# Edge counts made already turned, by ten small products a chunk, with rings of three one-hot pairs

## The reference

```python
cond = silu(emb @ f_w1 + f_b1) @ f_w2 + f_b2          # 1250 x 16, from sin/cos of a noise level
for i in range(4):
    y = cond_layer_norm(x, cond, ...)                  # scale and bias from cond
    q, k, v = y @ wq + bq, y @ wk + bk, y @ wv + bv    # 4 heads of 128
    scores = einsum('ehd,ehd->eh', q[src], k[dst])     # one score an edge and head
    out = segment_sum(softmax_over_src(scores) * v[dst], src)
    x = x + out @ wo + bo
    x = x + relu(cond_layer_norm(x, cond, ...) @ m_w1 + m_b1) @ m_w2 + m_b2
# graph convolution: h = (x @ W), normalised by sqrt of the degrees of both ends, summed over edges, twice
```

## Time and profile before

| what | us |
|---|---|
| median of 3 runs | 1870.88 |
| lowest and highest of the 3 | 1868.85, 1871.59 |
| the profiled execution | 1871.84 |
| its span in the trace | 1870.1 |
| PE busy, of the span | 1810.0 (97%) |
| PEld busy | 1575.5 (84%) |
| DVE busy | 1382.6 (74%) |
| ACT busy | 826.5 (44%) |
| POOL busy | 453.8 (24%) |

### The profile page before, as it was taken

The page is one execution under the profiler, slowest core; times in us unless marked ns, Lnnn a source line. Parts: engine busy times, 40 slices in busy tenths (PEclk is TensorE's granted clock), DMA queues, the critical chain, the costliest instruction groups (busy, mean ns, idle before and its releaser), DMA issues. The chain is left out here.

```text
span 1870.1 us, 33910 instructions
## 1 busy us (share of the span) xinstructions
PE 1810.0 (97%) x11814; PEld 1575.5 (84%) x11814; DVE 1382.6 (74%) x2847; ACT 826.5 (44%) x1613; POOL 453.8 (24%) x547
## 2 busy tenths in 40 slices
PE   6988999999999999999999999999999999999999
PEld 4656988999789889998898899988998999887877
DVE  8996668888875588888754988888549888885431
ACT  1552465555432255554322545544226545536220
POOL 2000333112341341113413411125134111262000
PEclk9999999999999999999999999999999999999999
DMA  4213462110300111113011211040112110522001
GB/s 143 55 41 79 141 176 91 38 43 27 123 24 34 58 42 39 38 31 124 4 54 42 58 38 38 27 128 1 46 50 61 38 38 27 142 72 55 1 1 55
DMA packets 50755, 108.43 MB, mean 58 GB/s; under 512 B 18170, under 2 KB 18222, under 8 KB 50640
## 3 DMA queue, kind: packets, MB, share of 16 engines
q1 hardware_dynamic: 50608, 106.87, 19.7%
q0 software_dynamic: 32, 0.03, 0.0%
HBM read 83.62 MB, written 23.25 MB: 57 GB/s over the span
## 5 line engine op out<-in xcount | busy, mean ns | idle before, releaser
L876 ACT ACTIVATE PT<-ps 125x500 fp32r<-125x500 f32 (+1 forms) x480 | 214.3, 520 | 315.1 <-PE ps L1790 315.1
L1690 PE MATMUL ps<-PT,V 125*128 125x250 f32 x2400 | 313.2, 284 | 1.7 <-DVE PT L1288 1.7
L1690 PE MATMUL ps<-kT,qg 128*125 128x512 f32 (+1 forms) x1440 | 302.1, 354 | 6.3 <-DVE nmx L1272 5.6
L1690 PEld LDWEIGHTS ps<-kT,qg 128*125 128x125 f32 x1440 | 245.4, 186 | 56.0 <-issue 6.9
L1690 PEld LDWEIGHTS ps<-PT,V 125*128 125x128 f32 x2400 | 289.6, 190 | 2.9 <-DVE PT L1288 2.9
L1288 DVE TENSOR_TENSOR PT<-ps,PT 125x500 fp32r<-125x500 f32 (+1 forms) x480 | 253.1, 582 | 2.1 <-ACT PT L876 1.7
L1272 DVE CUSTOM_DVE_ANT_0 SB<-ps,bt 125x1250 f32<-125x1250 f32 x140 | 203.9, 1457 | 47.4 <-PE ps L1690 44.6
L1790 PE MATMUL ps<-ident,pbuf 125*125 125x125 f32 x1600 | 202.2, 273 | 9.9 <-DVE PT L1288 4.0
L1790 PEld LDWEIGHTS ps<-ident,pbuf 125*125 125x125 f32 x1600 | 187.2, 189 | 13.6 <-issue 8.8
L870 ACT ACTIVATE pbuf<-SB,nmx 125x1250 f32<-125x1250 f32 x140 | 188.1, 1344 | 12.1 <-DVE nmx L1272 10.4
L1281 DVE TENSOR_SCALAR pbuf<-pbuf,rden 125x1250 f32<-125x1250 f32 x160 | 150.1, 938 | 5.6
(11 more groups left out here) (246 smaller groups left out, 2811.6 us busy)
## 6 DMA issues: line engine op xcount, KB each, us to landing
bt<-edge_bias_scratch SPq DMA_DIRECT2D x40, 546.9 KB
q_scratch<-qc SPq DMA_DIRECT2D x16, 500.0 KB, 2.6
qc<-q_scratch SPq DMA_DIRECT2D x16, 500.0 KB, 4.8
counts_scratch<-cblk SPq DMA_DIRECT2D x10, 546.9 KB
c_rows<-counts_scratch SPq DMA_DIRECT2D x10, 546.9 KB
edge_bias_scratch<-b_rows SPq DMA_DIRECT2D x10, 546.9 KB
counts<-counts_scratch SPq DMA_DIRECT2D x10, 546.9 KB
wm<-in_L_gnn_wo_dram SPq DMA_DIRECT2D x4, 1024.0 KB, 8.6
```

Source lines behind the costliest of these rows:

```text
L876: sc.activation(PT[:, h % 2, 0, a:b, u * T:(u + 1) * T], ps_T[0:T, i, 0:(b - a) * T].rearrange("p (t n) -> p t n", n=T), ACT.Copy).then_in ...
L1690: e = mm(out_, lhs(a), rhs(b), start=start and i == 0, stop=stop and i == 2)
```

## The change

The roles of the two one-hots are swapped. For each chunk, ten products have a 125-column block of `oh_src` as the stationary operand and `oh_dst` (125 columns) as the moving one, so the sums arrive already turned: sources on the partitions, destinations of the tile along the row. `ct`, the turning, its two banks and the semaphores `ct` and `ct_t` go. `oh_src` gets two more columns of ones, so the last block of each chunk has 126 rows and its last one sums to the number of edges of each destination; ScalarE copies it to `degT` and SyncE sends it through DRAM to `deg` (a store of 5 KB in the counting stage, and a load of 1250 single elements in the first layer). The rings hold three slots each and loops go in threes (21 chunks where a tile meets 19, 18 elsewhere). `split_wa_lo(1)` and `split_wa_lo(0)` leave the counting loop: the first goes after `yT_low(0)`, the second after `front_mod` in VectorE's first `project`. Several early buffers move to other places. `condition(i)` now waits for the evicted result before it, not for the turning.

```diff
-SIX = 6
-ECP = EC + SIX
+TRIO = 3
+ECP = EC + TRIO
...
+            sp.dma_start(deg_dram[0:1, :], degT[T:T + 1, :, :].rearrange("o t p -> o (t p)")).then_inc(s["deg_ld"], 16)
             for i in range(2):
                 sp.wait_ge(s[f"cnt_out{i}"], NT * 16)
...
                     for i in range(2):
                         sp.wait_ge(s[f"bst_out{i}"], NT * 16)
+                    sp.wait_ge(s["deg_ld"], 16)
+                    sp.dma_start(deg[:, :], deg_dram.rearrange("o (t p) -> p (o t)", p=T), allow_slow_non_contiguous=True).then_inc(s["deg_ld"], 16)
                     load_o(l)
...
+            g.memset(oh_src[:, :, N:N + 2], 1.0).then_inc(s["consts"], 1)
...
             for i in range(2):
                 pool.wait_ge(s[f"cnt_out{i}"], NT * 16)
+            pool.wait_ge(s["deg_ld"], 16)
...
-            def count_out(t):
+            def blocks_out(t):
                 act.wait_ge(s["ct_mm"], t + 1)
                 if t >= 2:
-                    act.wait_ge(s["ct_t"], AHEAD + 3 * (t - 1))
-                sc.activation(ct[t % 2], psf[0:T, ACC[t % 2]:ACC[t % 2] + N], ACT.Copy, accum_out=deg[:, t:t + 1]).then_inc(s["ct"], 1)
...
+                o = ACC[t % 2]
+                sc.activation(degT[96:T + 1, t, :], psf[96:T + 1, o + 1024 + T:o + 1024 + 2 * T], ACT.Copy)
                 for p, (a, b) in enumerate(PIECES):
-                    act.wait_ge(s["ct_t"], AHEAD + (t * 3 + p + 1))
-                    sc.activation(cblk[t % 2][:, a:b, :], ps_q[0:T, p % 2, 0:(b - a) * T].rearrange("p (t n) -> p t n", n=T),
+                    sc.activation(cblk[t % 2][:, a:b, :], psf[0:T, o + 512 * p:o + 512 * p + (b - a) * T].rearrange("p (t n) -> p t n", n=T),
                                   ACT.Copy).then_inc(s["ct_e"], 1)
...
-                with dve.Fori(0, sixes) as i:
+                with dve.Fori(0, trios) as i:
...
-                    for b in range(SIX):
-                        slot = ring * SIX + b
+                    for b in range(TRIO):
+                        slot = ring * TRIO + b
...
                 front_mod(f)
                 if first and n:
                     edge_bias(2 * n - 1)
+                if first and n == 0:
+                    split_wa_lo(0)
                 k_out(l, n)
...
-                if t in (4, 5, 6):
-                    split_wa_lo(6 - t)
+                if t == 4:
+                    split_wa_lo(2)
...
             yT_low(0, yTb)
+            split_wa_lo(1)
             layer(0, False, True)
...
-                    pe.wait_ge(s["ct"], AHEAD + t - 1)
+                    pe.wait_ge(s["ct_e"], AHEAD + 3 * (t - 1))
...
-                    for q in range(SIX):
-                        slot = ring * SIX + q
+                    for q in range(TRIO):
+                        slot = ring * TRIO + q
                         pe.wait_ge(s[f"onehot{ring}"], done + (q + 1))
-                        for a, b in COLS:
-                            e = mm(psf[0:T, o + a:o + b], oh_dst[:, slot, 0:T], oh_src[:, slot, a:b], start=False, stop=False,
-                                   skip_group_check=True)
+                        for p, (a, b) in enumerate(PIECES):
+                            for m in range(a, b):
+                                r = T + (m == NT - 1)
+                                e = mm(psf[0:r, o + 512 * p + (m - a) * T:o + 512 * p + (m - a + 1) * T],
+                                       oh_src[:, slot, m * T:m * T + r], oh_dst[:, slot, 0:T], start=False, stop=False, skip_group_check=True)
                         e.then_inc(s[f"oh_used{ring}"], 1)
...
-            pe.wait_ge(s["ct"], AHEAD + NT)
+            pe.wait_ge(s["ct_e"], AHEAD + 3 * NT)
             scale_bias(0, 0)
-            turn_counts(NT - 2, 2)
-            for p in range(3):
-                turn_counts(NT - 1, p)
             turn_y(0)
```

More of the change, by code:

```diff
@@ L229, in build @@
         cblk = [blocks(f"cblk{i}", [T, NT, T]) for i in range(2)]
-        ct = [blocks(f"ct{i}", [T, N])[:, :] for i in range(2)]
+        degT = blocks("degT", [T + 1, NT, T])
         in_wm = packer(r_wm, r_wm + 4 * 3 * KD * D)
@@ L471, in _ @@
             for ring in range(2):
-                pool.sem_inc(s[f"oh_used{ring}"], SIX)
+                pool.sem_inc(s[f"oh_used{ring}"], TRIO)
             g.memset(ident[:, :], 0.0).then_inc(s["ident"], 1)
@@ L1115, in one_hots @@
                                         edgeT[:, 1, bass.ds(chunk0 + b, 1)], None, ALU.is_equal)
-                        v.tensor_scalar(oh_src[:, slot, :], iota16[:, :], edgeT[:, 0, bass.ds(chunk0 + b, 1)], None,
+                        v.tensor_scalar(oh_src[:, slot, 0:N], iota16[:, :], edgeT[:, 0, bass.ds(chunk0 + b, 1)], None,
                                         ALU.is_equal).then_inc(s[f"onehot{ring}"], 1)
@@ L1615, in open_counts @@
             def open_counts(t):
                 if t >= 2:
-                    pe.wait_ge(s["ct"], AHEAD + t - 1)
-                for a, b in COLS:
-                    mm(psf[0:T, ACC[t % 2] + a:ACC[t % 2] + b], zeros16[:, 0:T], zeros16[:, 0:b - a], start=True, stop=False,
-                       skip_group_check=True)
-            def count_tile(t, sixes, before):
+                    pe.wait_ge(s["ct_e"], AHEAD + 3 * (t - 1))
+                for p, (a, b) in enumerate(PIECES):
+                    mm(psf[0:T + 1, ACC[t % 2] + 512 * p:ACC[t % 2] + 512 * p + (b - a) * T], zeros16[:, 0:T + 1], zeros16[:, 0:(b - a) * T],
+                       start=True, stop=False, skip_group_check=True)
@@ L1625, in count_tile @@
+            def count_tile(t, trios, before):
                 ring, o = t % 2, ACC[t % 2]
[L1626 to L1629 removed]
+                with pe.Fori(0, trios) as i:
+                    done = pe.snap((before + i) * TRIO)
+                    for q in range(TRIO):
+                        slot = ring * TRIO + q
                         pe.wait_ge(s[f"onehot{ring}"], done + (q + 1))
[L1631 to L1633 removed]
+                        for p, (a, b) in enumerate(PIECES):
+                            for m in range(a, b):
+                                r = T + (m == NT - 1)
+                                e = mm(psf[0:r, o + 512 * p + (m - a) * T:o + 512 * p + (m - a + 1) * T],
+                                       oh_src[:, slot, m * T:m * T + r], oh_dst[:, slot, 0:T], start=False, stop=False, skip_group_check=True)
@@ L1634, in count_tile @@
                         e.then_inc(s[f"oh_used{ring}"], 1)
                 following = trips(t + 1) if t + 1 < NT else None
-                for a, b in COLS:
-                    e = mm(psf[0:T, o + a:o + a + 2], zeros16[:, 0:T], zeros16[:, 0:2], start=False, stop=True, skip_group_check=True)
+                for p in range(3):
+                    e = mm(psf[0:T + 1, o + 512 * p:o + 512 * p + 2], zeros16[:, 0:T + 1], zeros16[:, 0:2], start=False, stop=True,
+                           skip_group_check=True)
@@ L1638, in count_tile @@
                 e.then_inc(s["ct_mm"], 1)
                 return following
-            def turn_counts(t, p):
-                a, b = PIECES[p]
-                if p == 0:
-                    pe.wait_ge(s["ct"], AHEAD + t + 1)
-                if p != 1:
-                    pe.wait_ge(s["ct_e"], AHEAD + 3 * t + p // 2)
-                for m in range(a, b):
-                    e = turn(ps_q[0:T, p % 2, (m - a) * T:(m - a + 1) * T], ct[t % 2][:, m * T:(m + 1) * T], ident[0:T, 0:T])
-                e.then_inc(s["ct_t"], 1)
@@ L1663, in condition @@
                 a, b = COLS[n]
[L1664 removed]
+                if 1 <= i <= 3:
+                    pe.wait_ge(s["h1"], i)
+                elif i > 3:
+                    pe.wait_ge(s["condT"], i - 3)
                 if i == 0:
@@ L1673, in _ @@
                 open_counts(t)
-                ahead = sixes_ahead(t)
-                if t >= 2:
-                    turn_counts(t - 2, 2)
+                ahead = trios_ahead(t)
                 if 2 <= t <= 7:
```

77 lines of the change are left out of this document (32 added, 45 removed).

## The result

The changed kernel takes **1874.0 us** (median of 11 runs, 1871.36 to 1875.62) against 1870.88 (11 runs, 1868.85 to 1871.6): ratio 1.0017, 95% interval 1.0009 to 1.0025. I had forecast 1865. The time lies inside the range of 1857 to 1876, but the sign is wrong: a small loss where I expected a gain of 6 us.

The account below looks back on a forecast made before the run. TensorE (97% busy) was taken to bound the run, with VectorE also near full in counting. Counting -7.7, joint +0.5, +1.2 and +0.4 gave -5.6, rounded to -6: 1865 us, range 1857 to 1876.

Parts of the forecast that it names:

- The product's price: Counting on TensorE: a 125-column bf16 load and product take 0.058 us a pair, 0.58 a chunk, under VectorE's 0.616.
- Rival A: Counting: a pair takes 0.077 us or more and TensorE carries the counting; 1887 us (1946 at 0.109); chance 0.12.
- the ring of three: Counting: a slot comes round in 1.85 us, 0.617 a chunk for three slots, as fast as VectorE itself.
- 0.5 where TensorE is late and three slots do not cover it: Counting: a deduction of 0.5 us from the 9.2 gained, leaving 8.7.
- 1.0 for the clock and the last tile: Counting: 1.0 us lost to slow-clock stretches and a late last tile, so counting ends 7.7 earlier.
- Rival B: Counting: short loops or three slots cost VectorE 0.2 us a trip, 12.4 over 62; gaps every three chunks; 1877; chance 0.08.
- Gains in counting: Counting: 0.9 us by tile 4's end, 3.7 from six dropped chunks, 4.6 from two dropped subtractions; 9.2 before losses.
- The six chunks' 3.7: Counting: VectorE drops six chunks of 192 at 0.616 us each, 3.7 us.
- The joint's copies: Joint: `degT` and three copies stand ahead of `scale_bias`, which starts about 2.2 us after the stop, +0.5.
- The joint's clock: Joint: with turning gone (it "hid nothing") TensorE idles; slow clock in first Q, 3.4 us, two chances in three, +1.2.
- `c_rows`: First layer: counts' rows arrive 5 us after issue, ScalarE waits; the 1.79 us won at `condc` is lost again, +0.4.
- `deg`: First layer: its 5 KB store and 1250-element load cost nothing, up to 3 us if weights queued behind are late.

Follow-up runs that it names:

- six_slots: Changed kernel with six slots in each ring and loops of six chunks (192 chunks in place of 186): 1868.13 us, ratio 0.999.
- slots_three_loops_six: Changed kernel with loops of six chunks (192 chunks) but still three slots in a ring: 1879.54 us, ratio 1.0053.
- products_only: Changed kernel with six slots, loops of six and the two subtractions back in counting, leaving the ten turned products alone: 1871.59 us, ratio 1.0011.
- fill_joint: Changed kernel with products of zeros on TensorE between the counting and the first Q: 1872.25 us, ratio 1.001.
- splits_early: Changed kernel with both moved subtractions one behind the other ahead of the first layer: 1872.46 us, ratio 1.0014.
- six_early: Changed kernel with six slots, loops of six chunks and both moved subtractions ahead of the first layer: 1865.97 us, ratio 0.9979.

## Why the prediction was wrong

**The product's price: right.** I took 0.058 a pair. Half of the f32 rows' 0.109 would have been 0.055; the 0.003 on top had no row behind it, and landed well. The rows give 0.057 to 0.060 at full clock; (2.45 - 0.313) / 20 = 0.107 in the half-clock stretch (21 products from 134.77). The Trainium skill's 81 ns ("TensorE: Matmul & The Clock Gate", "Back-to-back issue gap") does not hold for bf16 pairs of 125 columns here. Rival A fell.

**The step that failed: the ring of three.** I worked out a slot's round as 1.85 us, 0.617 a chunk, "as fast as VectorE itself". At full clock and in the middle of a tile this is so. But it left no slack, and I priced what then meets it at "0.5 where TensorE is late and three slots do not cover it", "about +0.5" in tile 0, and 1.0 for the clock and the last tile. What three slots cost measured 12.1 us by the ledger. In the terms of my sum, the products and the ring were to give 0.9 - 0.5 - 1.0 = -0.6 us; they gave 3.2 - 12.1 = -8.9. Nearly half of the 12.1 is a cycle I did not work out at the lower clock: a chunk takes TensorE 1.05 us there; six slots lend VectorE enough to pass a slow start (0.02 lost in tile 0 by before and by six_slots), three make it run at TensorE's pace from the fourth chunk on in tile 0. The rest is for the most part a tile's start: the 1.2 us at its head, which six slots partly hid, and then the wait for TensorE's first product.

**Rival B, which I gave 0.08,** named "the short loops or three slots", 0.2 us a trip, 12.4 us, 1877. The half of its name that says slots was right; the half that says trips was not (slots_three_loops_six). That its amount was all but right (12.1) is luck: it was a price for each of 62 trips, and the gaps at the turns of the loop, its own sign, come to 1.9 in tiles 4 to 9 at full clock. I had argued against it from the even 0.616 in the kernel before, which showed only that *six* slots keep VectorE even there.

**Gains in counting: right in kind.** With six slots VectorE begins tile 5 3.4 us earlier than before (80.46 against 83.85), and from its first to its last one-hot it needs 138.7 in place of 146.5 us: 7.8, of which 4.6 are the two subtractions and 3.2 the products. I had 0.9 for them behind three slots; the changed kernel's tile 5 starts 3.6 later (87.47). products_only stops 6.9 behind six_slots, the 4.6 and its slow clock. The six chunks' 3.7 are real, and are all that rings and loops of three bring: they cost 12.1.

**The joint's copies: right** (`scale_bias` 1.99 behind the stop; I had 2.2). **The joint's clock: right in kind, mis-sized.** I took one stretch of 3.4 us with two chances in three, +1.2. As priced it would have cost 1.7 if it came; it cost 2.75 in Q alone. The stretch was 10.2 us long (168.7 to 178.9) in the changed kernel's trace and in six others of the nine that let TensorE idle there (6.8 in two): 1.93 for 1.07 in turning, 8.62 for 5.87 in Q. The turning that "hid nothing" had a use: it kept the engine busy, and where zeros do so in its place (fill_joint) the stretch is gone.

**`c_rows`: right.** ScalarE waits for it at 192.05; landing took 4.83 us from issue where I took 5. (The 3.95 of that sum should be 3.98, twice 1.34 and 1.3, which changes nothing.) It took the place of the `condc` wait, so the move from Q to Q, without the 2.75 of slow clock, came to 23.38 - 2.75 = 20.63 against 20.64. splits_early, without that wait, needs 20.93 at a clock nearly as slow (Q 8.22 for 8.62): so the wait cost 2.0 in the trace, about as much as the `condc` wait before (1.79). **`deg`: right**, issued at 283.02; TensorE's longest wait for another engine from 280 to 300 is 1.1 us, as before, and the first reader of `deg` comes at 1353.

Sum by these terms, against before: counting 12.1 - 3.7 - 4.6 - 3.2 = +0.6 (trace 0.65); then 0.3 for the copies, 0.45 more until Q (it starts 8.53 behind the stop in place of 7.76), and 2.75 for Q itself: +4.1 at the second Q, where the trace has 196.09 - 191.93 = 4.2. It stays between 4.2 and 5.7 as far as 1740, for the most part at 4.4 to 4.8; 1.6 come back by the stretch there that did not occur, and that leaves the span's +2.9. Against the forecast, counting is 8.35 us short (7.7 earlier forecast, 0.65 later measured) and the joint 1.4 (2.1 and 3.5). This holds for one execution. Runs of one kernel spread over 4 us, and their mean granted clocks go with it: 0.994 or 0.995 in the four fastest of the changed kernel, 0.992 or 0.993 in the four slowest. Where their stretches fell is not recorded.

Open: why the time gained less from the joint's zeros on the changed kernel (1.3) than on six_early (3.2), where the traces give 3.6 and 3.1 from the stop to the second Q. Noise may be all of it; the runs' mean clocks go with it (median 0.994 to 0.995 there, 0.993 to 0.997 here). Open too: what places the late stretches, and why some pauses of TensorE are followed by a stretch and others are not.

## What to carry to other kernels

The depth of a ring is not there for the mean pace of its two ends but for the worst phase of either: work out a slot's round at TensorE's lower clock and at each loop's start, not only in steady state. Work that TensorE does off the critical path can be what holds its clock up for the chain behind it; where a change removes such work ahead of a wait, price the first long group after the wait at half speed. And when the counting's pace looks perfectly even, ask what makes it so before shrinking it.

## What was not expected of the hardware

- A pause of TensorE in the joint was followed by a half-clock stretch of 10.2 us in the changed kernel (163.00:178.00 at 0.69 above), not 3.4 as each in the kernel before; with the zeros (fill_joint) there was none.
- The windows' granted clock reads 1.00 in 13 to 22 us although products took a median of 314 ns against 221: where the clock's record has not begun, a product's own length is the better clock.
- At the start of a loop with two value loads VectorE stood 1.14 us with nothing to do ("<-issue" at 60.28); with six slots it was 0.77. How it divides between the loads and the loop no run here shows.
- Three f32 rows (0.107 to 0.109 us a pair) and a factor of two foretold a dense run of bf16 loads and products to 0.005 us: 0.055 against 0.057 to 0.060.
